# Reordering the start of the first expert slot: gate projections ahead of the logits, B u of block 1 inside the slot, and ScalarE's Q/K pieces ahead of its other work

## What is computed

```
h    = layernorm(x)*(1+ca) + sa;  n2 = layernorm(h)*ln_w + ln_b
data, gate = split(n2 @ W_in)             # 256 -> 384 + 384
u    = silu(causal_conv3(data))
Bu   = u @ Bm.T;  s_t = s_{t-1} @ M + Bu_t    # 16 states, a scan over the tokens
x2   = x + ga*(h + (sigmoid(gate) * (s @ Cm.T)) @ W_out)
h2   = layernorm(x2)*(1+cb) + sb
w    = softmax(routing(normalize(h2) @ normalize(sim) - sigmoid(gates)))   # n x 16 experts
q,k,v = sum_e w[:,e] * (h2 @ {q,k,v}_proj[e])     # 16 experts, 256 -> 128 each
out  = x2 + gb * sum_e w[:,e] * (attention(q,k,v) @ o_proj[e])
```

## Time and profile before

| | us |
|---|---|
| median of 3 runs | 1428.14 (1426.48 to 1429.53) |
| the profiled execution | 1428.48 |
| its span in the trace | 1426.7 |
| TensorE busy | 1376.8 |
| VectorE busy | 1151.5 |
| ScalarE busy | 675.1 |
| GpSimd busy | 706.4 |

### The profile page before, as it was taken

The page is one execution under the profiler, slowest core; times in us unless marked ns, Lnnn a source line. Parts: engine busy times, 40 slices in busy tenths (PEclk is TensorE's granted clock), DMA queues, the critical chain, the costliest instruction groups (busy, mean ns, idle before and its releaser), DMA issues. The chain is left out here.

```text
span 1426.7 us, 21069 instructions
## 1 busy us (share of the span) xinstructions
PE 1376.8 (96%) x6988; PEld 1219.8 (85%) x6988; DVE 1151.5 (81%) x2192; ACT 675.1 (47%) x1347; POOL 706.4 (50%) x636
## 2 busy tenths in 40 slices
PE   6898899999999999999999899999999999999997
PEld 4788899999999999999999777878787878878776
DVE  7876586785868767776678798989899999999866
ACT  4510302213013021040101298888888888888983
POOL 2421221312213013130114186888888888989897
PEclk9889999999999999999999999999999999999999
DMA  9000011100111010100227430000001000000000
GB/s 276 27 16 17 26 40 31 40 27 27 40 31 29 27 37 30 29 26 24 64 82 229 137 128 16 15 30 16 30 8 37 9 16 30 15 30 16 9 15 30
DMA packets 83133, 62.96 MB, mean 44 GB/s; under 512 B 13984, under 2 KB 75856, under 8 KB 82768
## 3 DMA queue, kind: packets, MB, share of 16 engines
q1 hardware_dynamic: 54880, 45.94, 10.3%
q10 hardware_dynamic: 28144, 15.67, 3.7%
HBM read 36.55 MB, written 25.03 MB: 43 GB/s over the span
## 5 line engine op out<-in xcount | busy, mean ns | idle before, releaser
L1731 PE MATMUL ps<-w_hi,memory_r 128*128 128x384 f32 x2048 | 566.8, 343 | 7.5 <-DVE wst L1440 7.5
L1440 DVE SCALAR_TENSOR_TENSOR wst<-ps,w_cur,wst 128x384 f32<-128x384 f32 x480 | 295.0, 615 | 158.8 <-PE ps L1731 146.0
L1731 PEld LDWEIGHTS ps<-w_hi,memory_r 128*128 128x128 f32 x2048 | 376.0, 189 | 11.8 <-DVE wst L1440 8.4
L1948 POOL TENSOR_TENSOR memory_rest<-memory_rest,pf 128x512 f32<-128x512 f32 x248 | 346.6, 1397 | 65.7 <-ACT pf L2055 57.4
L1731 PE MATMUL ps<-w_lo,memory_r 128*128 128x384 f32 x1024 | 344.5, 336 | 0.0
L2121 DVE TENSOR_TENSOR p_lo<-pf,p_hi 128x512 fp32r<-128x512 f32 x256 | 282.5, 1104 | 33.6 <-ACT p_hi L2057 32.4
L1731 PEld LDWEIGHTS ps<-w_lo,memory_r 128*128 128x128 f32 x1024 | 193.9, 189 | 4.7 <-issue 1.4
L2055 ACT ACTIVATE pf<-ps 128x512 f32<-128x512 f32 x256 | 153.1, 598 | 72.1 <-PE ps L2227 56.3
L2015 ACT COPY ps<-shift_rows 128x512 f32<-128x512 f32 x254 | 151.7, 597 | 5.9
L2057 ACT ACTIVATE p_hi<-ps 128x512 fp32r<-128x512 f32 x256 | 152.1, 594 | 0.0
L2102 DVE TENSOR_REDUCE mx<-ps 128x1 f32<-128x512 f32 x224 | 147.5, 678 | 1.2 <-PE ps L2216 1.2
(11 more groups left out here) (254 smaller groups left out, 2113.4 us busy)
## 6 DMA issues: line engine op xcount, KB each, us to landing
qk_scratch<-wst ACTq DMA_DIRECT2D x56, 128.0 KB, 2.2
x_scratch<-memory SPq DMA_DIRECT2D x8, 512.0 KB, 2.9
o_scratch<-memory_rest SPq DMA_DIRECT2D x16, 256.0 KB, 3.2
x2b<-x_scratch SPq DMA_DIRECT2D x32, 128.0 KB, 2.2
out_x<-memory_rest SPq DMA_DIRECT2D x32, 128.0 KB, 1.7
v_scratch<-wst ACTq DMA_DIRECT2D x60, 64.0 KB, 1.8
memory<-in_x SPq DMA_DIRECT2D x7, 512.0 KB, 4.0
memory_r<-qk_scratch SPq DMA_DIRECT2D x9, 256.0 KB, 4.9
```

What stands on the lines that cost most here:

```text
L1440: nc.vector.scalar_tensor_tensor(out=dst, in0=src, scalar=w, in1=dst, op0=ALU.mult, op1=ALU.add).then_inc(moe_acc, 1)
L1731: ins = nc.tensor.matmul(ps[:, s % MOE_BANKS, 0:H3], x_part[p][:, k, rows], w_part[:, k, e].rearrange("p t h -> p (t h)"), start=(k == 0 a ...
L1948: nc.gpsimd.tensor_tensor(p_sum[:, p], p_sum[:, p], pf[:, j % PB], ALU.add).then_inc(p_summed, 1)
```

## The change

TensorE's start-up ends in another order: data projections, h2 transposes, all three gate projections, logits. B u of block 1 moves into the first slot, one third after each of the steps 1, 2 and 3 (`FIRST_BU` is 1). VectorE forms u after the routing instead of in its middle, and the low part of the first tile of x ahead of the routing; `take_input` moves behind step 3, and the weight splits of experts 8 and 9 go into the slot (`LATE_SPLIT` 10 becomes 8: the split of expert 8+s follows step s). ScalarE copies `xt_hi[0]` earlier and takes the conv's sigmoid after the last gate. GpSimd's first low part waits for u instead of for the end of the routing. In the first slot alone, ScalarE takes Q/K/V of tile 0 ahead of `hidden` and those of tile 1 ahead of `gates_out`.

```diff
-        LATE_SPLIT = 10
+        LATE_SPLIT, FIRST_BU = 8, 1
@@ gpsimd @@
-                pool.wait_ge(dve_b, DVE_B + DVE_B_MORE)
+                pool.wait_ge(u_ready, FI + 1)
@@ scalar, pieces @@
+                    if first:
+                        high(0)
                     if ahead >= 2:
                         hidden(*a)
-                    high(0)
+                    if not first:
+                        high(0)
                     store(0)
                     if ahead >= 2:
                         data_out(*a)
+                    if first:
+                        high(1)
+                    if ahead >= 2:
                         gates_out(*a)
-                    high(1)
+                    if not first:
+                        high(1)
                     row_squares(*c)
@@ scalar, start-up @@
                 evacuate_projection(FI, FI + 1, 0, 1)
-                conv_sigmoid(0, 1)
+                evacuate_projection(FI + 1, FI + 2, 0, 1)
                 act.wait_ge(proj_mm, 4 * FI)
                 nc.scalar.copy(xt_hi[0], first_src).then_inc(h2t_ready, 1)
-                evacuate_projection(FI + 1, 2 * FI, 0, 1)
+                evacuate_projection(FI + 2, 2 * FI, 0, 1)
+                conv_sigmoid(0, 1)
                 exp(0, 0)
@@ vector @@
-                for n in range(3):
+                dve.wait_ge(h2t_ready, 1)
+                tt(xt_lo[0][:, :, 0:P], h2t[:, :, 0:P], xt_hi[0][:, :, 0:P].bitcast(F32), ALU.subtract
+                   ).then_inc(xlo_first, 1)
+                for n in range(ROUTE_PIECES - 1):
                     route_piece(n, 0, 0)
                 dve.wait_ge(csig_ready, 1 + FI)
                 tt(sg, sg, cv, ALU.mult).then_inc(u_ready, 1)
-                for n in range(3, 6):
-                    route_piece(n, 0, 0)
-                dve.wait_ge(h2t_ready, 1)
-                tt(xt_lo[0][:, :, 0:P], h2t[:, :, 0:P], xt_hi[0][:, :, 0:P].bitcast(F32), ALU.subtract
-                   ).then_inc(xlo_first, 1)
-                for n in range(6, ROUTE_PIECES - 1):
-                    route_piece(n, 0, 0)
-                take_input(0, 1, BU_BANK1)
-                split_w(8, LATE_SPLIT)
@@ vector, slot @@
+                        if is_first(i, p) and s == FIRST_BU + FI - 1:
+                            take_input(0, 1, BU_BANK1)
@@ tensor @@
                 h2_transposes(0, 0)
-                project(FI, 0, 1)
+                for f in range(FI, 2 * FI):
+                    project(f, 0, 1)
                 pe.wait_ge(dve_const, SIM_N)
                 logits_piece(0, 0)
-                for f in range(FI + 1, 2 * FI):
-                    project(f, 0, 1)
-                pe.wait_ge(proj_evac, 2 * FI + FI + 1)
-                for f in range(FI):
-                    first_input_term(f, 0, 1, BU_BANK1)
@@ tensor, slot, after the step's matmuls @@
+                        if is_first(i, p) and FIRST_BU <= s < FIRST_BU + FI:
+                            if s == FIRST_BU:
+                                pe.wait_ge(proj_evac, 2 * FI + FI + 1)
+                            first_input_term(s - FIRST_BU, 0, 1, BU_BANK1)
```

More of the change, by code:

```diff
@@ L904, in _, with pieces @@
                 nc.scalar.copy(st_parts[2 * CM_ROW:2 * CM_ROW + S, :], st_parts[0:S, :].bitcast(F32)).then_inc(st_hi_ready, 1)
-                def pieces(ahead, c, a, high, store):
+                def pieces(ahead, c, a, high, store, first):
+                    if first:
+                        high(0)
                     if ahead >= 2:
                         hidden(*a)
-                    high(0)
+                    if not first:
+                        high(0)
                     store(0)
@@ L955, in slot @@
                         pieces(ahead, following(i, p), (i + 1, p), lambda t: high_parts(i, p, t),
-                               lambda t: store_parts(i, p, t))
+                               lambda t: store_parts(i, p, t), is_first(i, p))
                     else:
```

## The result

The changed kernel takes 1420.29 us (median of 7, 1416.66 to 1422.88); before, in the same series, 1428.41 (median of 7, 1426.48 to 1430.95). The ratio is 0.9935, 95% interval 0.9921 to 0.9950: 7.1 to 11.3 us faster, middle 9.3. In another series the ratio was 0.9930 (0.9913 to 0.9946). The forecast of 1417.2 was 3.1 us too low against the first median and 0.6 us against the second (1417.84). The profiled execution took 1417.92, with a span of 1416.2.

The account below looks back on a forecast made before the run. The prediction took TensorE, busy 96% of the span, to bound the kernel nearly everywhere. Its terms, -7.1 - 4.5 + 0.3 = -11.3 us on 1428.48, gave 1417.2 us, with a range of 1414.5 to 1421.5.

Parts of the forecast that it names:

- rival 1: First slot's entry: the clock stays low through the whole interleaving of B u with steps; 3 us later, 1420.2; chance 0.28.
- Tile 0 ahead of n2: First slot, 124 us: taking Q and K earlier ends VectorE's wait and TensorE's idle and half-clock stretch; -7.1 us.
- Tile 1 ahead of the gates: First slot, 163 us: taking Q and K before the gates ends TensorE's waits for VectorE and h2; -4.5 us.
- The entry: First slot's start: TensorE stands 5.5 us for u, gains 0.4 by step 4, but VectorE's added splits eat it; +0.3 us.
- The port: Start of first slot: by the exclusion rule GpSimd's three products each hold a VectorE split, about 1 us worse.
- The shift should reach the end whole: After the first slot: TensorE-bound slots and attention follow without own deadline, so the whole -11.3 us arrives at the end.

Follow-up runs that it names:

- ScalarE's order alone: Kernel before the change, with only ScalarE's two moved Q/K/V pieces in the first slot and the old entry: 0.9923 and 0.9913 of before, 1416.51 and 1416.69 us.
- u early: Changed kernel, but VectorE forms u behind the third routing piece instead of the tenth: 0.9914 of before, 1416.80 us.
- B u one step later: Changed kernel with B u behind steps 2, 3 and 4 instead of 1, 2 and 3: 0.9934 of before, 1420.08 us.
- the entry alone: Changed kernel with ScalarE's old order in the first slot: 1.0005 of before, 1428.90 us.
- late splits: Changed kernel with only weight splits moved, expert 8 behind step 3 instead of step 0, and so on: 0.9929 of before, 1420.06 us.
- tile 0 alone: Kernel before the change, with only Q, K and V of tile 0 ahead of the n2 piece in the first slot: 0.9956 of before, 1421.42 us.

## Why the prediction was nearly right, step by step

The first median, 1420.29, is the number of rival 1 (1420.2) and not of the forecast. The number alone would have pointed to the wrong story; the trace and the two parts run alone speak for the forecast's terms.

- **Tile 0 ahead of n2, -7.1.** Right in the stage: -7.40 alone (of which 1.6 was lost again behind it, where tile 1's waits stayed). y came at 126.44 (forecast 126.45), no wait in front of it; the state parts ended at 120.8 (forecast 120.9).
- **Tile 1 ahead of the gates, -4.5.** Right in the stage: -4.2 to -4.55. Counting from starts was right, and the sum of the listed waits (3.8) too small: a wait is counted from the end of the last matmul's row. Between the starts of steps, at 1.04 us each, the three stalls of before (waits of 1.60, 1.19 and 0.99) cost 1.76, 1.48 and 1.26 us, together 4.5.
- **The entry, +0.3.** +0.33 measured, where 0.3 is scatter: what is shown is that it costs nothing near rival 1's 3 us. The stand of 5.5 us (5.44), the thirds (3.65, 2.02, 1.89 for 3.36, 1.8, 1.8), step 4's end (95.28 for 95.5) and the wait for the scan sum (1.06) came so. Rival 1, the low clock through the whole interleaving, came in none of three profiles. By whole times ScalarE's order alone (0.9923, 0.9913) lies 1 to 3 us below the changed kernel (0.9935, 0.9930); the intervals overlap, so a cost of the entry outside the stage is neither shown nor excluded.
- **The port.** The text beside the sum feared about 1 us. The three splits did lose 4.6 us (7.4 for 2.8), but in this kernel VectorE waited for TensorE behind step 3 and at step 4 all the same (0.25 and 0.88 us). By these rows nothing of the loss reached the end; no run takes the products out of this kernel, and a stage within 0.5 us of that of ScalarE's order alone agrees. With u early, where TensorE gets there sooner, the same products cost 5.8 us. The rule of the Trainium skill (SBUF — State Buffer, "Who interferes with whom") is that a VectorE tensor_tensor with both inputs in SBUF and a GpSimd instruction that reads SBUF exclude each other. The trace agrees: splits of 2.35 to 2.58 us for 0.94, each ending 0.8 us behind a product. The second and third product grew as well (3.07 and 2.87 for 2.35), since each of them in turn waited for a split.
- **The stage as a whole.** 99.73 - 11.3 = 88.4 forecast, 87.98 to 88.26 measured.
- **The rest.** "The shift should reach the end whole" is the step that failed in the profiled execution. At the end of the slots it was 11.9 us (808.73 to 796.83), at the end of the span 10.5. The forecast put the switch from the slots to attention at nothing; there the 1.4 us went. Rows of TensorE, before and then after:

```profile
808.73 0.33 PE L1647 MATMUL ps<-ident,wst 128*128 128x128 f32 x1 [0.71 <-DVE wst L1440]
...
811.54 0.47 PE L2225 MATMUL ps<-memory_r 128*128 128x512 f32 x1 [1.35 <-PEq L410]
815.38 0.47 PE L2225 MATMUL ps<-memory_r 128*128 128x512 f32 x1 [1.42 <-ACT ps L2015]
```

```profile
796.83 0.33 PE L1651 MATMUL ps<-ident,wst 128*128 128x128 f32 x1 [0.71 <-DVE wst L1442]
...
799.64 0.71 PE L2229 MATMUL ps<-memory_r 128*128 128x512 f32 x1 [1.35 <-PEq L410]
...
804.91 0.47 PE L2229 MATMUL ps<-memory_r 128*128 128x512 f32 x1 [1.39 <-ACT ps L2019]
```

The waits are the same, but the first score matmuls take 5.27 us instead of 3.84, and the windows give the clock:

```profile
800.00:802.00 2.00, 2.00 (x6) 1.54 (x6) 0.33 (x1) 0.33 (x1) 0.00 (x0) 0.50 0.62 182
```

The kernel with B u one step later shows 3.83 us there (802.34 to 806.17) and no low clock. From the slots' last transposes to the end of the span, before and the entry alone take 617.8 us, the changed kernel 619.0 to 619.3 in its three profiles, and ScalarE's order alone, one and the same program, 617.8 once and 619.3 once. So at least in part this belongs to the execution. Whether it comes more often in kernels with the shorter stage is open: the clock fell there in nine of the twelve profiles of kernels with ScalarE's new order or its first half, costing up to 1.5 us, and in neither of the two without.

- **The median.** Forecast 1417.2; measured 1420.29 and 1417.84. The stage explains none of the difference. As an estimate, 11.6 us in the stage less the 1.2 to 1.5 at the switch gives about 10.2, next to the 9.3 and 10.0 by ratio. Start-up (66.2 to 71.9 us over these profiles, 69.59 in the one that the forecast started from) and the switch (0 or 1.4) move an execution by several us; for instance the profiled execution with late splits took 1415.52 with a start-up of 66.22, where that kernel's median is 1420.06. More is not shown. The intervals of the two gains reach 11.3 and 12.4, so they hardly exclude the forecast's 11.3. That the second median lies 0.6 us from the forecast is in part luck.

## The better version

ScalarE's order with u early and late splits has the shortest stage of the versions that compute the whole result (85.86). By time it is 1416.68, 0.9913 of before; with an interval from 0.9895 to 0.9931 this can't be told from the changed kernel's 0.9930, nor from ScalarE's order alone (0.9913, 0.9923), which is the smallest edit and has all the gain.

## What to carry to other kernels

When an engine's in-order queue holds a short piece behind a long wait for something else, ask who waits for the short piece: two such reorderings on an engine that was 47% busy gave the bound engine 11.6 to 11.95 us, where 8.5 us of waits were listed; the rest fits the ends of the last matmuls and a stretch at half clock. Price a removed stall from the starts on both sides of it, not from the listed waits. Before filling or removing an idle stretch of the bound engine, look at what the next engine does in it; here VectorE needed the time, and three attempts to use it gave -0.8 to -1.1, 0 and +1.4 to +1.7 us, and only when VectorE's splits were moved away from the work of a third engine did it give -2.1 to -2.4. When one stall is removed alone, look behind the place where you measure: tile 0 alone lost 1.6 us again to a clock that fell later.

## What the runs showed of the hardware that was not expected

- The start-up up to block 0's h2 transposes, which the edits leave as it is, took 66.2 to 71.9 us over fourteen profiles, and 69.42 to 71.84 in three of one and the same kernel: more scatter than most edits here are worth.
- A split of 128x768 took 2.2 to 2.6 us beside a GpSimd product of 128x1024 and 0.94 without; a product behind such a split took 2.85 to 3.1 us instead of 2.35. Both pay, and they do it by turns: each split ended 0.8 us behind the end of a product, each such product 2.2 us behind the end of a split.
- The 48 matmuls of B u ran at the full level throughout when the stand before them was filled (1.97, 1.89, 1.89 us a third) and in block 0 (5.47 for all). Behind an idle stretch of 2.05 us they began at the full level, which fell 0.5 us later, and in one block they ran at half clock to their end (10.07 us), though TensorE was busy without a pause; it came back 4 us into the steps behind them. Broken up by steps, the clock was back after the first third and one step.
